# Query and key stacks of a two-layer attention kernel: part copies sent from SBUF to SBUF instead of through DRAM

## Chip, cores and metric

The kernel runs on one core of one Trainium2 chip. The metric is the device time of the whole launch in microseconds (us), the median of three runs.

## What is computed

The input is x with T = 1024 tokens and D = 256 features. There are two layers, each of the form x + attention(norm(x)) * silu(ffn(norm(x))).

```
layer 0: q = xn@Wq -> 16 heads x (q1,q2) of 16;  k = xn@Wk -> 4 kv heads x (k1,k2) of 16, rotary on all
         a_m = softmax(q_m k_m^T / 4 + causal mask), out = (a_1 - lam*a_2) v, group norm, @Wo
         ffn = mxfp4(xn) @ mxfp4(W)^T + bias
layer 1: q,k,v = xn@Wq, xn@Wk, xn@Wv -> 16 heads of 16, plain causal softmax attention, @Wo + bo
         ffn = gated mixture of 16 experts (top 4 of top 2 groups) of width 176, and a shared expert
```

A head's q1, q2, k1 or k2 is called a map here: 16 rows by 1024 tokens. Layer 0 has 32 query maps and 8 key maps, layer 1 has 16 and 16.

## The kernel before

**Stages.** The launch is a row of blocks, and each block ends when all engines have reached its end (a barrier; the wait shows in the profile at the line of the block's own statement: L231 for the first, L593 for an attention block, L981 for the middle one). The blocks are: the layer 0 projections (lines 231 to 393), the layer 0 attention (`attention`, 16 pairs of maps), `middle` (output projection, layer 0 ffn, second norm, layer 1 projections and routing), the layer 1 attention (8 pairs, the same function), and `experts`.

**Split parts.** Scores need fp32 accuracy from bf16 matmuls. Each fp32 projection value is cut into three bf16 parts (high, middle, low). The tile `stack0` (layer 1: `stack1`) holds for each map a column block of 1024 tokens and, in its partitions, six copies of 16 rows: for queries the parts 0, 1, 2, 0, 1, 0 (`QPARTS`), for keys the parts 0, 0, 0, 1, 1, 2 (`KPARTS`). One matmul over these 96 partitions gives all products of parts that count. Three more partitions hold the row maxima.

**Units.** The projections come in units (f, c): f is a group of 8 maps = 128 rows, c a half of the tokens. Layer 0 has ten units, in the order `UN`: the keys (f = 4) first, then queries f = 0 to 3, each with c = 0, 1. Layer 1 has eight (`UN1`). For each unit TensorE projects (L381) and swaps neighbouring rows with a permutation matrix `swp` (L371), VectorE multiplies with the rotary tables `rp` (L344, L346), GpSimd adds (L273), and ScalarE, VectorE and GpSimd cut the parts into a slot of `spl` (L302, L352, L305, L277; in layer 1 L1078, L1202, L1081, L1021). When the low part is done, the semaphore `lo_ok` rises.

**The way into the stack.** Everything that moves is a DMA from SyncE's queue, in program order. On `lo_ok` of a unit, `written` (L178) issues three DMAs from `spl` to a DRAM tensor (`part_scratch`, called `scr`; layer 1 `scr1`): 384, 256 and 128 KB, 768 KB in 1 KB rows. When both halves of a group are written, `gathered` (L182) reads the group back from DRAM into 96 partitions of the stack, with the rows and maps exchanged on the way: `near_maps` the first two maps (384 KB), `far_maps` the other six (1152 KB). In the block of the projections these reads are issued after units 2 and 3 for groups 4 and 0; the rest is issued during the attention's first pairs, from `late`, behind the three small DMAs of `rows` (L833). In layer 1 the groups 2 and 0 are read after the fourth unit and groups 3 and 1 during pairs 0 and 1. TensorE waits in `loaded` for what a pair needs.

**Other names.** `outputs` (L446, L447, L453, L454) copies the attention's results from SBUF to SBUF, 32 or 16 partitions at a time, and single rows with them. SLOTS = 8 slots of `spl` in layer 0, SPL = 5 in layer 1; ScalarE waits for the DMAs of a slot's last use (`unit_written`) before it writes the slot again.

Of the kernel before, what the change touches and what calls it, by code (L numbers as in the profile page):

```python
# [18 lines left out]
BF16 = mybir.dt.bfloat16  # L19
# [4 lines left out]
P = 128  # L24
# [48 lines left out]
def program(nc, x, wq, wk, wv, wo, lams, gnw, gnb, fw, fb, wq1, wk1, wv1, wo1, bo, gate,  # L73
# [46 lines left out]
    with ctx:  # L120
        ps = ctx.enter_context(nc.psum_tensor("ps", [P, 8, 512], F32))
        psb = ps[:, :, :].bitcast(BF16)
        scr = nc.dram_tensor("part_scratch", [5 * P, 6, T], BF16, kind="Internal").ap()
        scr1 = nc.dram_tensor("part_scratch1", [4 * P, 6, T], BF16, kind="Internal").ap()
# [29 lines left out]
        stk0 = [sem(f"stk0_{f}") for f in range(5)]  # L154
        stk1 = [sem(f"stk1_{f}") for f in range(4)]
        near0 = [sem(f"near0_{f}") for f in range(5)]
# [29 lines left out]
        def wait_written(sp, layer, f):  # L186

            for c in range(NC):
                sp.wait_ge(*unit_written(layer, (UN, UN1)[layer].index((f, c))))
# [4 lines left out]
        def near_maps0(sp, f):  # L194

            wait_written(sp, 0, f)
            gathered(sp, stack0, at0(f), scr, f, 0, 2, near0[f])

        def far_maps0(sp, f):

            gathered(sp, stack0, at0(f), scr, f, 2, 8, stk0[f])


        with ExitStack() as a:
# [10 lines left out]
            qf = sb("qf", [P, 2, 512], F32)  # L215
            lm = sb("lm", [P, 4, DH], F32)
# [13 lines left out]

# [1467 lines left out]
```

## Time and profile before

| | |
|---|---|
| median of three runs | 868.28 us (868.22 to 869.21) |
| the profiled execution: its own time, its span | 868.93 us, 867.2 us |
| mean granted TensorE clock | 0.92 |
| busy: TensorE, weight loads, VectorE, ScalarE, GpSimd | 762.9, 365.0, 529.4, 432.3, 430.6 us |
| DMA of the data queue | 69.15 MB in 60016 packets |
| writes to part_scratch | 18 of 384 KB, 18 of 256 KB, 18 of 128 KB |
| reads from part_scratch | 9 of 384 KB, 9 of 1152 KB |

The span runs from the first to the last instruction of the profiled execution; 1.7 us of its own time lie outside. Lines such as L178 are lines of the kernel. SPq is SyncE's issue of DMAs: its duration is the time for which the issue holds the queue, not the time of the transfer. PEq and POOLq are the sequencers of TensorE and GpSimd.

### The profile page before, as it was taken

Reading aid. Unit: us, or ns where it says so; the run is one execution under the profiler, and the core shown is the slowest. Engines: PE = TensorE matmul, PEld = TensorE weight load, DVE = VectorE, ACT = ScalarE, POOL = GpSimd, SP = SyncE. Lnnn points to the kernel's source line nnn. Section 1 sums busy time; section 2 is a strip of 40 time slices with the busy share of each in tenths; the row PEclk is TensorE's granted clock in tenths of the full one; section 3 lists DMA queues with packets and bytes.
Section 4 is the critical chain, followed back from the end, with each engine's and each line's share of the span. In section 5 each row is a group of like instructions: output and inputs, shape, how many; then the busy total and the mean of one; then the engine's idle time right before and its main releaser. Section 6 shows DMA issues by size and latency. Waiting matters only on the chain. (4 is left out here: it accounts for less than half of the span.)

```text
span 867.2 us, 12855 instructions
## 1 busy us (share of the span) xinstructions
PE 762.9 (88%) x3632; PEld 365.0 (42%) x3632; DVE 529.4 (61%) x1441; ACT 432.3 (50%) x922; POOL 430.6 (50%) x751
## 2 busy tenths in 40 slices
PE   3938999999999999965984889999669999999995
PEld 2322222222222223222651222322148888888884
DVE  3649787778777768223653867886035555555555
ACT  1431666666666556732141256666534555455552
POOL 1751566654244324321222123334276999799994
PEclk9985999999999999975996698999969999999997
DMA  5393630110020011012059552432221212122221
GB/s 182 130 299 87 154 87 15 43 43 14 20 63 15 21 40 38 21 44 60 1 179 261 129 141 66 126 98 69 87 87 43 66 60 67 52 62 71 62 64 55
DMA packets 60075, 69.83 MB, mean 81 GB/s; under 512 B 14904, under 2 KB 40857, under 8 KB 60010
## 3 DMA queue, kind: packets, MB, share of 16 engines
q1 hardware_dynamic: 60016, 69.15, 28.4%
q8 instruction: 24, 0.39, 0.2%
q14 instruction: 35, 0.29, 0.1%
HBM read 47.35 MB, written 15.47 MB: 72 GB/s over the span
## 5 line engine op out<-in xcount | busy, mean ns | idle before, releaser
L675 ACT ACTIVATE top<-ps 128x512 f32<-128x512 f32 (+3 forms) x384 | 171.0, 490 | 132.4 <-PE ps L622 132.2
L605 PE MATMUL ps<-mid 96*128 96x512 bf16 (+3 forms) x576 | 191.2, 356 | 29.0 <-PEq L981 11.8
L709 DVE CUSTOM_DVE_ANT_0 ps<-ps,keep 128x512 f32<-128x512 f32 (+3 forms) x384 | 184.2, 504 | 41.9 <-PE ps L605 41.2
L622 PE MATMUL ps<-mid 99*128 99x512 bf16 (+3 forms) x576 | 185.7, 338 | 9.2 <-ACT mid L675 6.3
L1450 PE MATMUL ps<-xp,wp 128*128 128x512 f32 (+1 forms) x600 | 149.6, 400 | 14.3 <-ACT wp L1502 8.8
L642 PE MATMUL ps<-top,mid 128*33 128x512 f32 (+3 forms) x768 | 161.6, 500 | 0.0
L622 PEld LDWEIGHTS ps<-mid 99*128 99x128 bf16 x576 | 54.3, 99 | 185.8 <-ACT top L675 103.0
L1450 PEld LDWEIGHTS ps<-xp,wp 128*128 128x128 f32 (+1 forms) x600 | 115.0, 192 | 40.3 <-ACT xp L1504 9.3
L791 POOL TENSOR_SCALAR_AFFINE_SELECT top<-top 128x128 f32<-128x128 f32 x256 | 71.5, 294 | 109.4 <-ACT top L675 107.0
L675 ACT ACTIVATE mid<-ps 128x512 f32<-128x512 f32 (+1 forms) x192 | 82.6, 492 | 69.9 <-PE ps L622 41.8
L713 DVE TENSOR_REDUCE top<-ps 128x1 f32<-128x512 f32 x128 | 88.4, 691 | 36.0 <-PE ps L605 35.5
L1622 DVE SCALAR_TENSOR_TENSOR a<-th,ps 128x512 f32<-128x512 f32 (+1 forms) x50 | 34.4, 688 | 91.1 <-ACT th L1520 91.1
L605 PEld LDWEIGHTS ps<-mid 96*128 96x128 bf16 x576 | 58.2, 102 | 75.3 <-issue 30.1
L1466 PE MATMUL ps<-gp,w2p 128*128 128x512 f32 (+1 forms) x300 | 77.7, 395 | 2.0 <-POOL gp L1572 2.0
L1552 POOL TENSOR_TENSOR wp<-top,wp 128x512 fp32r<-128x512 f32 (+1 forms) x50 | 64.6, 1293 | 27.9 <-ACT wp L1502 27.9
L1572 POOL TENSOR_TENSOR gp<-g,gp 128x512 fp32r<-128x512 f32 (+1 forms) x50 | 64.6, 1292 | 8.8 <-ACT gp L1533 2.6
L791 POOL TENSOR_SCALAR_AFFINE_SELECT mid<-mid 128x128 f32<-128x128 f32 x128 | 36.2, 293 | 63.3 <-ACT mid L675 60.1
L1533 ACT CAST gp<-g 128x512 fp32r<-128x512 f32 (+1 forms) x50 | 31.1, 622 | 68.3 <-DVE g L1631 68.3
L1466 PEld LDWEIGHTS ps<-gp,w2p 128*128 128x128 f32 (+1 forms) x300 | 57.0, 191 | 14.4 <-POOL gp L1572 2.5
L1568 POOL TENSOR_TENSOR w2p<-top,w2p 128x256 fp32r<-128x256 f32 (+1 forms) x50 | 57.5, 1151 | 2.7 <-ACT w2p L1530 2.7
L642 PE MATMUL ps<-mid 128*17 128x512 f32 (+3 forms) x384 | 55.0, 512 | 0.0
L713 DVE TENSOR_REDUCE mid<-ps 128x1 f32<-128x512 f32 x64 | 44.1, 689 | 16.2 <-PE ps L605 16.1
(199 smaller groups left out, 777.7 us busy)
## 6 DMA issues: line engine op xcount, KB each, us to landing
mid<-part_scratch SPq DMA_DIRECT2D x9, 1152.0 KB, 8.6
part_scratch<-top SPq DMA_DIRECT2D x18, 384.0 KB, 5.1
top<-in_w SPq DMA_DIRECT2D x16, 396.0 KB, 4.0
cw_s<-combine_rows SPq DMA_DIRECT2D x48, 128.0 KB, 3.0
part_scratch<-top SPq DMA_DIRECT2D x18, 256.0 KB, 5.2
mid<-part_scratch SPq DMA_DIRECT2D x9, 384.0 KB, 3.9
top<-inverse_scratch SPq DMA_DIRECT2D x12, 256.0 KB
top<-in_w SPq DMA_DIRECT2D x8, 384.0 KB, 5.4
```

The lines of the kernel that those rows point to most:

```text
L605: nc.tensor.matmul(ps[:, s_bank(turn), 0:w], queries(pair, m)[0:PARTS, i * P:(i + 1) * P], keys(pair, m)[0:PARTS, c * 512:c * 512 + w], st ...
L622: nc.tensor.matmul(ps[:, ST_BANK + n % AHEAD, 0:w], keys(pair, m)[0:STACK, j * P:(j + 1) * P], queries(pair, m)[0:STACK, q0:q0 + w], start ...
L642: nc.tensor.matmul(ps[r0:r0 + dv, ACC + c, q0 - 512 * c:512], v, pr[:, n % RING, 0:w], start=start, stop=stop).then_inc(multiplied, 1)
L675: nc.scalar.activation(pr[:, n % RING, 0:w], ps[:, ST_BANK + n % AHEAD, 0:w], ACT.Exp, scale=0.25).then_inc(p_ready, 1)
L709: ins = nc.vector.tensor_tensor_reduce(bank, bank, msk[:, 512 - w:512], -1.0 if low else 1.0, 3e38 if low else -3e38, ALU.add, ALU.min if ...
L713: ins = nc.vector.tensor_reduce(mx[:, m, i - 4, c:c + 1], bank, AX.X, ALU.max)
L791: nc.gpsimd.affine_select(out=square, in_=square, pattern=[[1, P]], compare_op=ALU.is_ge, fill=0.0, base=0, channel_multiplier=-1).then_in ...
L1450: last = nc.tensor.matmul(ps[0:r, bank + b, :], wp[:, b, pw, w + kk, 0:r], xp[:, px, kk, c * 512:(c + 1) * 512], start=j == 0 and kk == 0, ...
L1466: last = nc.tensor.matmul(ps[:, YB + kk, :], w2p[0:r, b, pw, kk * P:(kk + 1) * P], gp[0:r, b, pg, :], start=first and j == 0, stop=final a ...
L1552: nc.gpsimd.tensor_tensor(wp[:, b, 1, :, 0:r], w13[:, :, :, bass.ds(i * P, r)].rearrange("p w c n -> p (w c) n"), wp[:, b, 0, :, 0:r].bitc ...
L1568: nc.gpsimd.tensor_tensor(w2p[0:r, b, 1, :], w2s[0:r, bass.ds(i, 1), :].rearrange("p i d -> p (i d)"), w2p[0:r, b, 0, :].bitcast(F32), ALU ...
L1572: nc.gpsimd.tensor_tensor(gp[0:r, b, 1, :], g[0:r, b, :], gp[0:r, b, 0, :].bitcast(F32), ALU.subtract).then_inc(gl_ok, 1)
```

## The change

The DRAM tensors and the gathers are gone. `written` now sends six DMAs for each unit, one for each copy of a part: its 128 partitions go into 16 partitions by 8 maps of the stack, 1 KB for each row and map, 128 KB in all. A DMA walks the source's partitions in order, so the projection's rows must come as (row in the map, map) and not as (map, row). For this GpSimd reorders the columns of the weights once they are loaded (`regrouped`: one copy of 128 x 256 elements for the keys and four for the queries in layer 0, four in layer 1). The raw weights are loaded into tiles that are not in use yet (`r1`, `qf`, layer 1 `r11`). The rotary tables are loaded as 16 rows repeated for 8 maps, in two DMAs instead of one. The permutation matrix is made by VectorE from the identity (two copies of 128 x 64) instead of loaded. All waits for gathers become waits for the six DMAs of the units: TensorE waits for a whole group at the first pair that needs it, and SyncE waits for all units at the start of each attention (`early0`, `early1`) before it issues anything there.

```
-        scr = nc.dram_tensor("part_scratch", [5 * P, 6, T], BF16, kind="Internal").ap()
-        scr1 = nc.dram_tensor("part_scratch1", [4 * P, 6, T], BF16, kind="Internal").ap()
...
-            return scr_ok[slot], 48 * (before + v // SLOTS + 1)
+            return scr_ok[slot], 96 * (before + v // SLOTS + 1)
...
-        def written(sp, to, f, c, parts, is_key, done):
-            rows = to[f * P:(f + 1) * P, :, c * 512:(c + 1) * 512]
-            for first_row, width, part in ((0, 3, 0), (3, 2, 1), (5, 1, 2)):
-                if is_key:
-                    of = parts[:, part, :].unsqueeze(1).to_broadcast([P, width, 512])
-                else:
-                    of = parts[:, 0:width, :]
-                sp.dma_start(rows[:, first_row:first_row + width, :], of).then_inc(done, 16)
-        def gathered(sp, stack, at, of, f, lo, hi, done):
-            sp.dma_start(stack[0:PARTS, at + lo:at + hi, :],
-                         of[f * P + 16 * lo:f * P + 16 * hi, :, :].rearrange("(m r) n t -> (r n) m t", r=16)
-                         ).then_inc(done, 16)
+        def written(sp, stack, at, c, parts, is_key, done):
+            for n, part in enumerate(KPARTS if is_key else QPARTS):
+                sp.dma_start(stack[16 * n:16 * n + 16, at:at + 8, c * 512:(c + 1) * 512], parts[:, part, :]).then_inc(done, 16)
...
+        def by_row(w):
+            return w.rearrange("p k (m r) -> p k r m", r=16)
+        def regrouped(pool, to, of, f, done):
+            cols = slice(f * P, (f + 1) * P)
+            nc.gpsimd.tensor_copy(to[:, :, cols].rearrange("p k (r m) -> p k r m", r=16), by_row(of[:, :, cols])).then_inc(done, 1)
...
+            wk_raw = r1[:, 0, 0:KD * P].rearrange("p (k n) -> p k n", k=KD)
...
+            def turned(v):
+                return v[:, :].rearrange("p (a b m) -> p a b m", b=2, m=8)
...
-                    sp.dma_start(swp[:, :], swap).then_inc(ld_c, 16)
-                    for t, w in ((wk_s, wk), (wv_s, wv), (wq_s, wq)):
+                    for t, w in ((wk_raw, wk), (qf, wq), (wv_s, wv)):
-                    sp.dma_start(rp[:, :, :], rope.rearrange("m p t -> p m t")).then_inc(ld_r, 16)
+                    for m in range(2):
+                        sp.dma_start(rp[:, m, :], rope[m, 0:16, :].unsqueeze(1).to_broadcast([16, 8, T])).then_inc(ld_r, 16)
...
-                        written(sp, scr, f, c, spl[:, u % SLOTS, :, :], f == 4, scr_ok[u % SLOTS])
-                        if u == 2:
-                            near_maps0(sp, 4)
-                        if u == 3:
-                            near_maps0(sp, 0)
-                            far_maps0(sp, 0)
+                        written(sp, stack0, at0(f), c, spl[:, u % SLOTS, :, :], f == 4, scr_ok[u % SLOTS])
...  GpSimd, layer 0, after the norm's rstd
+                    pool.wait_ge(ld_w, 16 * 3)
+                    regrouped(pool, wk_s, wk_raw, 0, v_clr)
+                    for f in range(4):
+                        regrouped(pool, wq_s, qf, f, v_clr)
...  VectorE, layer 0
-                    dve.wait_ge(ld_c, 48)
+                    dve.wait_ge(ld_c, 32)
+                    for odd in range(2):
+                        nc.vector.tensor_copy(turned(swp)[:, :, odd, :], turned(idf)[:, :, 1 - odd, :]).then_inc(ids, 1)
...
-                            late(sp, pair)
+                        early(sp)
                         ahead(0)
...
+                wait_written(pe, 0, 4)
             if pair % 4 == 0:
-                pe.wait_ge(near0[pair // 4], 16)
-            if pair % 4 == 1:
-                pe.wait_ge(stk0[pair // 4], 16)
+                wait_written(pe, 0, pair // 4)
+        def early0(sp):
+            for f in range(4):
+                wait_written(sp, 0, f)
...
+            if pair % 4 == 0:
+                wait_written(pe, 1, 2 + pair // 4)
+                wait_written(pe, 1, pair // 4)
+        def early1(sp):
+            sp.wait_ge(comb_kept, 16)
+            for f in range(4):
+                wait_written(sp, 1, f)
...  middle: SyncE, then GpSimd
-                    sp.dma_start(wqk[:, :, n * D:(n + 1) * D], w.rearrange("(c p) n -> p c n", p=P)).then_inc(ldw, 16)
+                    sp.dma_start(r1[:, :, n * D:(n + 1) * D], w.rearrange("(c p) n -> p c n", p=P)).then_inc(ldw, 16)
-                    written(sp, scr1, f, c, spl[:, u % SPL, :, :], f >= 2, scr_ok[u % SLOTS])
-                    if u == EARLY - 1:
-                        near_maps1(sp, 2)
-                        near_maps1(sp, 0)
-                        far_maps1(sp, 2)
-                        far_maps1(sp, 0)
+                    written(sp, stack1, 8 * f, c, spl[:, u % SPL, :, :], f >= 2, scr_ok[u % SLOTS])
+                pool.wait_ge(ldw, 64)
+                for f in range(4):
+                    env["regrouped"](pool, wqk, r1, f, v_clr)
                 pool.wait_ge(stats, 3)
```

## Rows read from the trace of the kernel before

**Rows 1.** Stages: us, busy of PE, PEld, DVE, ACT, POOL, clock, DMA share, GB/s
```profile
0.00:63.70 63.70, 34.36 (x108) 18.16 (x109) 29.57 (x63) 21.33 (x38) 30.34 (x30) 0.94 0.64 200
378.80:470.50 91.70, 60.71 (x248) 37.95 (x249) 40.51 (x152) 23.86 (x50) 22.37 (x35) 0.76 0.38 107
```

**Rows 2.** Timeline, end of the first block and start of attention 0
```profile
55.03 1.15 POOL L277 TENSOR_TENSOR top<-top 128x512 bf16<-128x512 f32 x1
...
63.72 4.45 PE L605 MATMUL ps<-mid 96*128 96x128 bf16 x14 [11.05 <-PEq L231]
```

**Rows 3.** Timeline of SyncE's queue, layer 0 (start, us held, line)
```profile
32.31 7.67 SPq L178 DMA_DIRECT2D part_scratch<-top  x9
...
47.23 15.85 SPq L178 DMA_DIRECT2D part_scratch<-top  x18
```

**Rows 4.** The same writes to DRAM grouped by line, 30 to 64 us
```profile
DMA to landing us min/median/max: 2.5/5.2/9.7
```

**Rows 5.** Stretches, columns as in rows 1: queue saturated; narrow copies alone
```profile
57.00:63.00 6.00, 0.00 (x0) 0.00 (x0) 0.00 (x0) 0.00 (x0) 0.00 (x0) 0.50 1.09 384
...
549.40:553.20 3.80, 3.80 (x24) 1.15 (x21) 3.18 (x8) 2.72 (x6) 0.00 (x0) 1.00 0.13 28
```

**Rows 6.** Timeline of SyncE's queue, middle block
```profile
440.32 10.26 SPq L178 DMA_DIRECT2D part_scratch<-top  x12
...
456.60 13.03 SPq L178 DMA_DIRECT2D part_scratch<-top  x12
469.68 0.31 SPq L1001 DMA_DIRECT2D combine_rows<-top  x1
```

**Rows 7.** Timeline, end of the middle block and start of attention 1
```profile
459.10 2.26 POOL L1021 TENSOR_TENSOR top<-top 128x512 bf16<-128x512 f32 x2 [0.80 <-ACT top L1081]
...
470.51 4.45 PE L605 MATMUL ps<-mid 96*128 96x128 bf16 x14 [11.76 <-PEq L981]
```

**Rows 8.** SBUF-to-SBUF DMAs by line: issue min/median/max ns, and time to landing
```profile
L453 SPq DMA_DIRECT2D keep<-keep x24: 507/589/593, 509.5 to 627.5; - x24
DMA to landing us min/median/max: 1.9/2.1/10.1
...
L454 SPq DMA_DIRECT2D keep<-keep x32: 585/589/1180, 510.0 to 628.2; - x32
DMA to landing us min/median/max: 1.7/1.8/9.7
```

**Rows 9.** Timeline of SyncE's queue: one load, and two copies back to back
```profile
4.88 0.47 SPq L241 DMA_DIRECT2D mid<-in_fw  x1
...
549.64 0.59 SPq L454 DMA_DIRECT2D keep<-keep  x1
550.27 0.59 SPq L453 DMA_DIRECT2D mid<-keep  x1
```

**Rows 10.** Timeline of SyncE's queue, pairs 1 to 4 of attention 0
```profile
95.67 2.32 SPq L833 DMA_DIRECT2D mid<-top  x3
...
114.12 2.21 SPq L833 DMA_DIRECT2D mid<-top  x3
...
132.59 1.78 SPq L833 DMA_DIRECT2D mid<-top  x3
...
151.04 1.78 SPq L833 DMA_DIRECT2D mid<-top  x3
```

**Rows 11.** Timeline, GpSimd around the new copies, and TensorE's first projection
```profile
18.15 3.96 PE L381 MATMUL ps<-keep,top 128*128 128x512 f32 x8
...
24.38 1.26 POOL L273 TENSOR_TENSOR top<-top 128x512 f32<-128x512 f32 x1 [11.30 <-DVE top L346]
...
404.43 1.05 POOL L1013 TENSOR_TENSOR top<-top 128x4 f32<-128x4 f32 x1 [4.50 <-DVE top L1129]
```

**Rows 12.** One GpSimd line with one input, by line; one VectorE row of layer 0
```profile
L803 POOL TENSOR_SCALAR top<-top x5: 614/614/616, 93.9 to 167.6; 128x512 f32<-128x512 f32 x5
...
35.71 1.67 DVE L352 TENSOR_TENSOR top<-top 128x512 f32<-128x512 f32 x1 [0.37 <-POOL top L277]
```

More of the change, by code:

```diff
@@ L152, in program @@
         dqw = sb("dqw", [P, 2, D], BF16, mid)
-        stk0 = [sem(f"stk0_{f}") for f in range(5)]
-        stk1 = [sem(f"stk1_{f}") for f in range(4)]
-        near0 = [sem(f"near0_{f}") for f in range(5)]
         unit_near = sem("unit_near")
@@ L330, in _ @@
                                                 ALU.subtract, ALU.mult).then_inc(normed, 1)
-                    dve.wait_ge(ld_r, 80)
+                    dve.wait_ge(ld_r, 96)
                     for n in range(2):
@@ L369, in swapped @@
                     def swapped(u):
+                        if u == 0:
+                            pe.wait_ge(ids, 3)
                         pe.wait_ge(qs_ok, u + 1)
@@ L379, in _ @@
                         w, o = (wk_s, 0) if f == 4 else (wq_s, f * P)
+                        if c == 0:
+                            pe.wait_ge(v_clr, 2 if f == 4 else 3 + f)
                         for k in range(KD):
@@ L393, in _, with attention @@
                             last.then_inc(v_mm, 1)
-        def attention(layer, stack, vall, N, loaded, late):
+        def attention(layer, stack, vall, N, loaded, early):
             first = layer == 0
@@ L877, in loaded0 @@
                 pe.wait_ge(unit_near, 16)
-                pe.wait_ge(near0[4], 16)
-            if pair == 4:
-                pe.wait_ge(stk0[4], 16)
+                wait_written(pe, 0, 4)
             if pair % 4 == 0:
-                pe.wait_ge(near0[pair // 4], 16)
-            if pair % 4 == 1:
-                pe.wait_ge(stk0[pair // 4], 16)
-        def late0(sp, pair):
-            if pair == 0:
-                far_maps0(sp, 4)
-            if pair < 3:
-                near_maps0(sp, pair + 1)
-                far_maps0(sp, pair + 1)
+                wait_written(pe, 0, pair // 4)
+        def early0(sp):
+            for f in range(4):
+                wait_written(sp, 0, f)
         o0, combined0, last_inverses0, last_inverted0, last_scaled0, last_combined0 = attention(
-            0, stack0, v0, 16, loaded0, late0)
+            0, stack0, v0, 16, loaded0, early0)
         mid[1] = 0
@@ L897, in program @@
         stack1 = sb("stack1", [P, 32, T], BF16, mid)
-        def near_maps1(sp, f):
-            wait_written(sp, 1, f)
-            gathered(sp, stack1, 8 * f, scr1, f, 0, 2, unit_near)
-        def far_maps1(sp, f):
-            gathered(sp, stack1, 8 * f, scr1, f, 2, 8, stk1[f])
         middle(nc, locals())
@@ L915, in loaded1 @@
             if pair == 0:
-                pe.wait_ge(unit_near, 16 + 3 * 16)
-            if pair == 4:
-                pe.wait_ge(unit_near, 16 + 5 * 16)
-            if pair % 4 == 1:
-                pe.wait_ge(stk1[2 + pair // 4], 16)
-                pe.wait_ge(stk1[pair // 4], 16)
-        def late1(sp, pair):
-            if pair == 0:
-                sp.wait_ge(comb_kept, 16)
-            if pair < 2:
-                near_maps1(sp, (3, 1)[pair])
-                far_maps1(sp, (3, 1)[pair])
+                pe.wait_ge(unit_near, 16 + 16)
+            if pair % 4 == 0:
[5 more added lines that the diff above has]
+                wait_written(sp, 1, f)
         o1, combined1, last_inverses, last_inverted, last_scaled, _ = attention(
-            1, stack1, v1, 8, loaded1, late1)
+            1, stack1, v1, 8, loaded1, early1)
         mid_c.close()
@@ L940, in middle @@
         env[n] for n in ("idf", "mv", "st6", "rst", "ve", "mhalf", "wo_s", "gnc"))
-    v1, stack1, scr1, idb, comb = (env[n] for n in ("v1", "stack1", "scr1", "idb", "comb"))
+    v1, stack1, idb, comb = (env[n] for n in ("v1", "stack1", "idb", "comb"))
     st6o, dqa, dqw, row_stats = (env[n] for n in ("st6o", "dqa", "dqw", "row_stats"))
@@ L978, in middle @@
         UN, scr_ok, unit_written, unit_near = (env[n] for n in ("UN1", "scr_ok", "unit_written", "unit_near"))
-        written, near_maps1, far_maps1 = env["written"], env["near_maps1"], env["far_maps1"]
+        written = env["written"]
         EARLY = 4
@@ L1288, in _ @@
                         pe.wait_ge(ldw, 64)
+                        pe.wait_ge(v_clr, 2 + 4)
                     if t >= 3:
```

11 lines of the change are left out of this document (4 added, 7 removed).

## Prediction

> **What bounds the kernel now.** I read the stages first, then both ends of the two stages that the change touches, and only then the queue that does the moving. The projections of layer 0 take 63.7 of 867.2 us and the middle block 91.7 us [rows 1]; everything else keeps its instructions. In the first block the last unit's low part is done at 55.03 + 1.15 = 56.18 us, and yet the first matmul of attention 0 starts at 63.72, after 11.05 us in which TensorE had nothing [rows 2]. The compute engines wait there for one thing, SyncE's queue: its last write to the scratch is issued at 47.23 + 15.85 = 63.08 [rows 3]. The queue itself is held by the transfers. 18 DMAs take 15.85 us, 0.88 us each, where a load is issued in 0.47 us [rows 3, 9]; the DMA engines are full at 384 GB/s while nothing else runs [rows 5], and a write lands 5.2 us after its issue [rows 4]. The same picture stands at the end of the middle block: last part done at 459.10 + 2.26 = 461.36, queue done at 469.68 + 0.31 = 469.99, TensorE starts at 470.51 after 11.76 us of idleness [rows 6, 7]. So about 7 us and 8.5 us of the time are queue alone. Both are on the path, and a change that shortens or lengthens the queue moves the end of the launch one for one, until the units' own times (56.2 and 461.4) become the bound.
>
> **What the change removes.** All reads from scratch, 1536 KB for each of nine groups, go. Three groups' worth of them, or parts, stand in the queue before the barriers; the others lie in the attention. Those in the attention are covered: the row maxima go out at 95.67, 114.12, 132.59 and 151.04, so the pairs take 18.45, 18.47 and 18.45 us, the first two with gathers behind the maxima and the third without [rows 10]. I count no gain there. The traffic ahead of the barriers halves, so the full DMA engines are no longer what holds the queue, if the new writes go at the old rate.
>
> **What it adds: six issues for each unit in place of three.** There are 60 in layer 0 and 48 in layer 1, all of 128 KB from SBUF to SBUF. The trace has no such DMA. The nearest rows are the SBUF-to-SBUF copies of the attention, which hold the queue for 0.59 us in the median whatever they carry, 32 KB (L453) or 2 KB (L454) [rows 8], and start 550.27 - 549.64 = 0.63 us apart back to back [rows 9]. The other neighbour is a load with 128 partitions, 0.47 us, or 0.51 with the same 0.04 us between two [rows 9]. I take 0.63, as source and target are both in SBUF, and keep 0.51 as the lower bound. Upward I take 0.70, the copy's price and some of what a fuller queue adds.
>
> Layer 0: the first unit comes at 32.31 and the units come every (56.18 - 32.31) / 9 = 2.65 us. Six issues take 6 x 0.63 = 3.8 us, so after the first unit the queue never runs empty. It ends at 32.31 + 60 x 0.632 = 70.2 where it ended at 63.1: +7.1 us. The first pair needs only the first four units, issued by 32.31 + 24 x 0.632 = 47.5, so it waits for the barrier and not for data.
>
> Layer 1: the first four units need 24 issues, 15.2 us from 440.32 to 455.5, and are through before the fifth comes at 456.60 [rows 6]. The other four take 15.2 us from there, to 471.8, and the combine rows 0.3: 472.1 against 469.99, +2.1 us.
>
> **The regroupings.** A GpSimd instruction with one input over 512 elements takes 614 ns [rows 12]. For 256 elements read with a stride the bounds are 0.3 us (half of it) and 1.2 us (four times that); I take 0.6. Layer 0: GpSimd sits idle for 11.30 us before 24.38 [rows 11], so from 13.08; the key weights are ready at 13.7 (at most 14.3) and TensorE first wants them at 18.15 [rows 11]; all five are done at 16.1, at most 19.1. Middle: GpSimd sits idle for 4.50 us before the power at 404.43 [rows 11], which is on the path; four copies take 2.4 us, at most 4.8. So 0, and +0.3 us at the upper bound. If the cover were gone it would be 2.4 us. There is a second way to pay. A VectorE row next to GpSimd work, both reading SBUF, took 1.67 us [rows 12], and tiny VectorE steps of the group norm now run beside the four copies. I enter +0.2 us for it, between 0 and 1.
>
> **The rest.** The swap matrix is no longer loaded, one issue of 0.47 us less ahead of VectorE's start, and two copies of 128 x 64 elements more on VectorE; together about 0, between -0.3 and +0.3. The second rotary DMA is one issue of 0.47 us in a queue whose tables are first used after 18.15. SyncE's wait for all units at the start of an attention stands ahead of the row maxima, which were issued about 14 us after the attention's start; the last unit lands about 5 us after its issue at most, if that is as slow as the full queue's median [rows 4], so nothing behind it is late. ScalarE's wait for a slot comes eight units after the slot's last use, five in layer 1: the tightest is the last unit there, whose slot was issued until 440.32 + 18 x 0.632 = 451.7 and is wanted shortly before 459. Both hold only as long as the transfers keep up with the queue. TensorE's granted clock is already 0.50, its lower level of 1.2 GHz, in the wait before attention 0 [rows 5], so a longer wait adds its length and no lower clock.
>
> **Sum.** 7.1 + 2.1 + 0.2 = 9.4 us. The profiled execution takes 868.93 us by its own time (span 867.2), the median is 0.65 less: 878.3 for it, 877.7 for the median; I say 878.
>
> **Rival 1: the narrow target is the bound.** Each DMA writes into 16 partitions only. L453 does that with 32 KB and lands 2.1 us after issue; L454 beside it moves 2 KB and lands after 1.8 [rows 8]. 30 KB more for 0.3 us is 100 GB/s, a quarter of the 384 of [rows 5]. In the stretch that holds those copies alone the engines are busy 13% of the time for 28 GB/s, 215 GB/s at full share [rows 5], though such short copies hardly overlap. At 100 GB/s a DMA takes 1.3 us, at 215 it takes 0.6, just the issue interval. It decides from 0.63 us, that is below 207 GB/s. At 1.3 us the 60 DMAs of layer 0 need 78 us from 32.3, to 110, and the queue ends 5 to 10 us ahead of that, as far as it ran ahead of its landings before [rows 4]: about +39. The 48 of layer 1 need 62 us from 440.3, to 503, or about +20 with the wait ahead of the row maxima: about 927 in all. Against it: consecutive DMAs go to different partitions, so engines that have drifted apart can use several targets at once. A half-way 0.9 us gives 32.3 + 54 - 6 = 80 (+17) and 440.3 + 43 - 3 = 480 (+10): 895.
> The Trainium skill (SBUF — State Buffer, "Door 1: The DMA port swizzle") says that a transfer's rate depends on how many of 16 ports its partitions reach, and that 16 partitions reach four, measured at 104 GB/s. By that a DMA would take 1.26 us, as in the slow form of this rival; the landing times of this trace agree (100 GB/s).
>
> **Rival 2, the other sign: the queue is freed.** Without gathers and with half the traffic the queue may go at the price of an issue alone, and that may be smaller than the copies'. At 0.51 us layer 0 ends at 32.3 + 30.6 = 62.9 (-0.2) and layer 1 at 456.6 + 12.2 + 0.3 = 469.1 (-0.9): 867, no difference that can be told. It decides from 0.51 down. At 0.45 us layer 0 ends at 59.3 and layer 1 at 467.7: -3.8 and -2.3, 862. For it: a load's price is close to this. Against it: every SBUF-to-SBUF row stands at 0.59 us.
>
> **Rival 3: nothing to see.** Rival 2 at 0.51, or a gain in one layer and a loss in the other.
>
> **Chances and range.** A run of this kernel can tell 0.2%, 1.7 us, from no change. The forecast (issue-bound, 0.57 to 0.70 us): 0.52. Its own range is 872 (0.57: 66.5 and 470.6, +4.1) to 884 (0.70: 74.3 and 474.2, +15.4). Rival 1: 0.27, two thirds of it below 900, as the drift helps. Rival 2 with a gain: 0.12. Rival 3: 0.09. The range 867 to 900 leaves out the faster cases and the slow third of rival 1. Faster 0.12, same 0.09, slower 0.79.
>
> **What the profile after would show.** If I am right: in SyncE's queue 60 writes from 32.3 to about 70, one row, each held 0.59 us, and 24 from 456.6 to 472; landing within 3 us; TensorE's first L605 matmuls at about 70.8; DMA share well below full with the queue still busy. Rival 1: issues held for 1 us and more, landing after 5 to 12 us, DMA share near full at 100 to 200 GB/s. Rival 2: issues of 0.47 us or less and TensorE starting before 63.7. The regroupings are right if the power at L1013 comes no later after VectorE's L1129 than before. The prediction fails above all if the price of an issue depends on the shape in a way that these rows don't show, or if narrow targets share a path.

## Result: 2.6% slower, and where the 21 us lie

The changed kernel takes 891.12 us (888.76 to 893.13) against 868.25 us of the kernel before on the same chip: a ratio of 1.0261, 95% interval 1.0233 to 1.0288. The forecast was 878. Its direction held and its size did not: the loss is 22.9 us and not 9.7.

The profiled execution after has a span of 888.7 us, 21.5 more than before. I cut both executions at the same four events: the first score matmul of attention 0, the first part transfer of layer 1, the first score matmul of attention 1, and the first gather of the experts.

| stretch | before | after | difference |
|---|---|---|---|
| start to attention 0 | 63.72 | 83.87 | +20.2 |
| attention 0 and the middle block up to the first part transfer | 376.60 | 377.97 | +1.4 |
| part transfers of layer 1 to attention 1 | 30.19 | 37.14 | +7.0 |
| attention 1 to the first gather of the experts | 159.35 | 153.15 | -6.2 |
| experts | 237.34 | 236.57 | -0.8 |

The +1.4 of the second row says little: the same stretch takes 375.8 us in the execution of run 10 below and 378.2 in that of run 12.

Stretches of the kernel after, with the columns of [rows 1] and of [rows 5]: the block of the projections, the middle block, the time in which only the queue is left, and attention 1:

```profile
0.00:83.70 83.70, 34.42 (x108) 18.14 (x108) 31.04 (x65) 21.33 (x38) 33.34 (x34) 0.84 0.85 123
399.80:498.70 98.90, 60.82 (x248) 38.10 (x248) 41.22 (x152) 24.00 (x50) 24.59 (x39) 0.74 0.48 65
55.00:83.00 28.00, 0.00 (x0) 0.00 (x0) 0.79 (x3) 1.70 (x4) 2.38 (x2) 0.55 1.16 132
498.70:652.00 153.30, 137.05 (x776) 39.07 (x776) 105.18 (x340) 88.64 (x208) 47.19 (x165) 0.91 0.36 92
```

TensorE's own work is what it was (34.42 us against 34.36 in [rows 1]); the block is longer by waiting. From 55 to 83 us the DMA engines are full (share 1.16), as they were in [rows 5], but they move 132 GB/s where they moved 384. Busy DMA engines at a third of the rate are the main finding: the share alone would say that nothing changed.

The timeline after, end of the first block and start of attention 0, which answers to [rows 2]:

```profile
53.31 4.07 POOL L267 TENSOR_TENSOR top<-top 128x512 bf16<-128x512 f32 x3
53.59 29.15 SPq L168 DMA_DIRECT2D mid<-top  x30
...
83.87 2.72 PE L601 MATMUL ps<-mid 96*128 96x128 bf16 x9 [30.01 <-PEq L220]
```

The last 30 transfers take 29.15 us to issue, 0.97 each, and TensorE idles for 30.01 us where it idled for 11.05. Grouped by line, all 60 of layer 0 (issue min/median/max in ns, first and last start, then issue to landing), which answers to [rows 4]:

```profile
L168 SPq DMA_DIRECT2D mid<-top x60: 597/627/1962, 33.5 to 82.0; - x60
...
DMA to landing us min/median/max: 3.4/14.7/16.8
```

The first transfer lands 3.4 us after its issue, the median one 14.7. While the queue has room the issues go out 0.65 us apart, as the forecast had it, and the transfers land 1.06 us apart (36.88, 37.99, 39.05, 40.12). One issue is held for 0.98 us at 45.28, but the next 14 go out 0.64 to 0.69 us apart again. From 55.5 us on, with 16 or 17 transfers under way, nearly every issue is held until a transfer has landed. The last is issued at 81.95 and lands at 96.46.

SyncE's queue in the middle block, which answers to [rows 6], and attention 1's start, which answers to [rows 7]:

```profile
461.84 35.78 SPq L168 DMA_DIRECT2D mid<-top  x48
497.66 0.45 SPq L972 DMA_DIRECT2D combine_rows<-top  x1
514.54 1.83 SPq L829 DMA_DIRECT2D mid<-mid  x3
```
```profile
484.88 2.26 POOL L995 TENSOR_TENSOR top<-top 128x512 bf16<-128x512 f32 x2 [5.06 <-ACT top L1055]
...
498.98 6.34 PE L601 MATMUL ps<-mid 96*128 96x128 bf16 x18 [18.70 <-PEq L957]
```

The last transfer lands at 512.63. SyncE's wait for all units ends there, and VectorE has the row maxima ready at 513.10, so this wait doesn't hold them up. They go out at 514.54, 15.6 us after the attention's start and not 14.2 (484.66 against 470.51 before); the profile puts the last 1.4 us to the DMA of the combine rows, which stood behind the transfers, but doesn't show why. The delay cost no time that can be seen: the next maxima go out 31.1 us after the attention's start, and 30.9 before.

The slots of `spl` ran out as well. ScalarE waits 5.1 us for the transfers of a slot in the middle block:

```profile
483.70 0.59 ACT L1052 CAST top<-ps 128x512 bf16<-128x512 f32 x1 [5.11 <-DMA mid<-top]
```

The last low part is done at 484.88 + 2.26 = 487.14, 25.3 us after the first transfer where it was 21.0 before. The queue ends 11 us later still, so this wait is covered too.

**The start.** The first part transfer goes out at 33.52, 1.2 us later than in [rows 3]. Timelines of 12 to 20 us, the kernel after and then the kernel before:

```profile
13.10 3.09 POOL L185 COPY top<-top 128x256 f32<-128x256 f32 x5
13.25 4.05 DVE L321 TENSOR_SCALAR top<-keep 128x256 f32<-128x256 f32 x8 [2.21 <-POOL keep L251]
```
```profile
13.19 2.67 DVE L329 TENSOR_SCALAR top<-keep 128x256 f32<-128x256 f32 x8 [2.21 <-POOL keep L267]
```

The five regroupings take 3.09 / 5 = 0.62 us each, and VectorE's eight normalisations beside them take 4.05 us and not 2.67. The transposes behind them start 1.15 us later (15.86 against 14.71). In all executions of full kernels the eight normalisations take 4.05 or 4.06 us where the copies run beside them and 2.67 where they don't. At the first transfer the difference is blurred: the kernel before and runs 2, 8, 9 and 12, whose code is the same up to there, have it between 32.31 and 33.22.

**What came back.** In the kernel before, SyncE issues the gathers of groups 3 and 1 in the first two pairs of attention 1, and right behind them, as in every pair of this attention, three loads of expert weights (`in_w`, 1176 KB). Its timelines and its stretches there:

```profile
503.30 1.01 SPq L182 DMA_DIRECT2D mid<-part_scratch  x2
504.35 1.02 SPq L841 DMA_DIRECT2D top<-in_w  x2
505.41 0.50 SPq L844 DMA_DIRECT2D top<-in_w  x1
```
```profile
517.12 0.58 ACT L685 COPY mid<-ps 64x512 f32<-64x512 f32 x1 [2.48 <-DMA keep<-mid]
```
```profile
506.00:511.00 5.00, 5.00 (x34) 1.57 (x32) 3.85 (x12) 3.66 (x10) 2.29 (x8) 1.00 1.06 234
511.00:516.00 5.00, 4.48 (x26) 1.32 (x22) 4.34 (x15) 2.55 (x5) 0.44 (x2) 1.00 1.02 284
516.00:521.40 5.40, 3.16 (x13) 0.58 (x14) 0.97 (x5) 2.46 (x5) 0.44 (x2) 0.61 0.01 3
521.40:530.00 8.60, 8.60 (x39) 2.54 (x38) 5.19 (x16) 4.18 (x11) 2.68 (x10) 0.65 0.47 150
```

Gathers and weights fill the DMA engines from 506 to 516, the small output copies behind them land up to 10 us after their issue [rows 8], ScalarE waits for the buffer that they empty, TensorE is idle for 2.2 of 5.4 us, and its granted clock falls to its lower level, 0.50, from 517.2 to 527.5 (so the means of 0.61 and 0.65 in the last two stretches). The row maxima of attention 1's pairs are 16.7, 20.0 and 18.5 us apart before, and 15.5, 16.2 and 15.9 after, where the weight loads go on as they were.

### The profile page after: what moved, and what is told of

The parts are those of the page before. It is cut to its first block and busy times, and to the rows that moved or that the text cites. A ratio compares the mean times of both kernels' runs of the same rounds, so it can differ in the third digit from the quotient of the medians.

```text
span 888.7 us, 12906 instructions
## 1 busy us (share of the span) xinstructions
PE 758.5 (85%) x3632; PEld 363.2 (41%) x3632; DVE 531.4 (60%) x1443; ACT 431.8 (49%) x922; POOL 435.7 (49%) x760
## 5 line engine op out<-in xcount | busy, mean ns | idle before, releaser
L1425 PE MATMUL ps<-xp,wp 128*128 128x512 f32 (+1 forms) x600 | 149.2, 399 | 14.5 <-ACT wp L1477 8.8
L1527 POOL TENSOR_TENSOR wp<-top,wp 128x512 fp32r<-128x512 f32 (+1 forms) x50 | 64.6, 1292 | 27.7 <-ACT wp L1477 27.7
L1508 ACT CAST gp<-g 128x512 fp32r<-128x512 f32 (+1 forms) x50 | 31.1, 622 | 68.5 <-DVE g L1606 68.5
L1441 PEld LDWEIGHTS ps<-gp,w2p 128*128 128x128 f32 (+1 forms) x300 | 56.2, 188 | 14.2 <-POOL gp L1547 2.5
```

The lines of the kernel that those rows point to most:

```text
L1425: last = nc.tensor.matmul(ps[0:r, bank + b, :], wp[:, b, pw, w + kk, 0:r], xp[:, px, kk, c * 512:(c + 1) * 512], start=j == 0 and kk == 0, ...
L1441: last = nc.tensor.matmul(ps[:, YB + kk, :], w2p[0:r, b, pw, kk * P:(kk + 1) * P], gp[0:r, b, pg, :], start=first and j == 0, stop=final a ...
L1527: nc.gpsimd.tensor_tensor(wp[:, b, 1, :, 0:r], w13[:, :, :, bass.ds(i * P, r)].rearrange("p w c n -> p (w c) n"), wp[:, b, 0, :, 0:r].bitc ...
```

## Experiments

**1. The shapes by themselves.** A kernel of DMAs alone, from a 128-partition SBUF tile with 1 or 2 KB for each partition, and no computation:

```
for i in range(18): sp.dma_start(dst[16n:16n+16, 8 maps, 512], src[:, 0:512])      # the kernel's shape and order
for i in range(8):  sp.dma_start(dst[0:32, 8 maps, 512], src as [128, 2, 512])     # and 0:16, 0:64, all 128, DRAM
```

> Only DMAs, no attention: series of equal transfers from one SBUF tile of 128 partitions, one series after the other; the output is zeros. Theory (the narrow target is the bound): 128 KB into 16 partitions land 1.0 to 1.1 us apart in the order of the kernel and 1.2 us apart in the order 0, 2, 1, 3, 4, 5 of the copies; the same split over two queues lands under 0.9 us apart; 256 KB land 2.4 us apart when all go into partitions 0 to 15, 2.0 us when they alternate between partitions 0 to 15 and 64 to 79, 1.2 us for 32 and for 64 partitions alike, 0.7 us for 128 partitions; from DRAM into 16 partitions about 2.1 us, as from SBUF. Rival A (any SBUF-to-SBUF transfer is slow, the source counts): 256 KB into 128 partitions land 2.1 us apart too, and from DRAM into 16 partitions 0.7 us. Rival B (the issue is the bound): everything of 128 KB lands 0.65 us apart.

Stretches of it (DVE and POOL, clock, DMA share, GB/s), in this order: the kernel's shape; 256 KB to 16 partitions; to 32; to 64; to 128; from DRAM to 16:

```profile
8.00:24.00 16.00, 0.00 (x0) 0.00 (x0) 1.00 1.11 117
70.00:90.00 20.00, 0.00 (x0) 0.00 (x0) 1.00 1.06 117
123.00:138.00 15.00, 0.00 (x0) 0.00 (x0) 1.00 1.04 130
141.00:157.00 16.00, 0.00 (x0) 0.00 (x0) 1.00 1.00 131
160.00:165.00 5.00, 0.00 (x0) 0.00 (x0) 1.00 1.02 381
173.00:190.00 17.00, 0.00 (x0) 0.00 (x0) 1.00 0.95 123
```

The kernel's shape lands every 1.06 us with nothing else in the program, and the issue is not what holds it. By line, the kernel's shape and the same 128 KB to all 128 partitions:

```profile
L41 SPq DMA_DIRECT2D dst<-src x18: 579/608/687, 3.6 to 14.7; - x18
...
DMA to landing us min/median/max: 3.4/7.0/10.4
```
```profile
L79 SPq DMA_DIRECT2D dst<-src x12: 472/601/603, 190.9 to 197.9; - x12
...
DMA to landing us min/median/max: 2.0/2.1/2.1
```

Same bytes, same issue of 0.6 us; one falls behind by 7 us in 18 transfers ((14.7 + 10.4 - 3.6 - 3.4) / 17 = 1.06 us each), the other never (0.64 us apart, the issue). So the narrow target is the bound, and that the source lies in SBUF is not, since DRAM to 16 partitions is as slow (2.06 us for 256 KB). Two things that I had counted on don't help: 256 KB always to partitions 0 to 15 take 2.27 us each, and alternating between 0 to 15 and 64 to 79 2.17; and from two queues at once the pair together gives the same 1.06 us per transfer, where I had expected less than 0.9. In the order 0, 2, 1, 3, 4, 5 of the copies it is 1.15 us (1.2 expected). The expected 1.2 us for 256 KB into 32 and 64 partitions didn't come: they take 2.02 and 1.92.

**2 and 3. One layer at a time.** The kernel before with the direct transfers in layer 1 alone, and in layer 0 alone:

```
+ direct(sp, stack1, 8 * f, c, ...)       - written(sp, scr1, f, c, ...), near_maps1, far_maps1      # 2
+ written(sp, stack0, at0(f), c, ...)     - near_maps0, far_maps0; layer 1 as before                 # 3
```

> The kernel before with the change made in layer 1 alone. Theory (the slow copies hold the middle block's queue about 7 us longer, and the gathers that are gone had cost attention 1 about 6.5 us in its pairs 2 and 3): 867 to 870 us, attention 1 at least 5 us shorter than before, its start 6 to 8 us later. Rival (the gathers in the attention were covered, as the prediction has it; attention 1 got shorter for another reason, such as the clock): 874 to 876 us.

> The changed kernel with layer 1 put back to the DRAM scratch, layer 0 direct. Theory (nearly all of the loss is layer 0's queue, ending 19 to 20 us later, and its start 1.2 us later): 888 to 892 us, attention 0 starting at 83 to 85 us, attention 1 as long as before. Rival (layer 1 costs its share too, as in the prediction's 7 to 2): 882 to 886 us.

Layer 1 alone gives 873.61 us, ratio 1.0049 (1.0035 to 1.0062), layer 0 alone 887.17, ratio 1.0211 (1.0185 to 1.0238). Together that is +22.6 us, and the whole change is +22.9: the parts add up. In layer 1 alone the stretch of the part transfers is 38.6 us (30.2 before) and attention 1 takes 153.5 (159.3): a loss of 8.4 and a gain of 5.8 that mostly hide each other. Attention 1 was shorter as the theory had it, but it starts 11.1 us later and not 6 to 8, 2.7 of it from before the first part transfer, and so the time lies above the theory's 867 to 870. Run 3 lies just below its 888 to 892. Its attention 0 starts at 84.31, as expected; its attention 1 takes 157.0 us and not as long as before, although its gathers are back; why is open.

**4. The regroupings after the normalisation.**

```
+ pool.wait_ge(normed, NT)
  regrouped(pool, wk_s, wk_raw, 0, v_clr)
```

> The changed kernel, but GpSimd starts its weight copies in layer 0 only when VectorE has written all eight normalised tiles. Theory (the copies hold VectorE back while both read SBUF, and that is the first unit's 1.2 us): first write issued at about 32.4 us instead of 33.5 and a time 1.0 to 1.4 us under the changed kernel's. Rival (the later start comes from the loads): no change, 33.5 us.

The timeline of its queue and its GpSimd copies:

```profile
32.53 3.89 SPq L168 DMA_DIRECT2D mid<-top  x6
```
```profile
16.07 2.85 POOL L185 COPY top<-top 128x256 f32<-128x256 f32 x5 [2.94 <-DVE top L322]
```

The normalisations take 2.67 us again and the transposes start at 14.78, 1.1 us earlier. The first transfer goes out at 32.53, 1.0 us earlier, and attention 0 starts at 82.80, 1.07 us earlier. The time is 890.83 (ratio 1.0249, 1.0227 to 1.0270) against a ratio of 1.0261 (1.0233 to 1.0288): the microsecond is in the trace and can't be told in the times.

**5 and 11. More shapes.**

> Only DMAs, one shape after another, no computation; 256 KB each unless said. The first such run gave 2.0 to 2.2 us per 256 KB for targets of 16, 32 and 64 partitions and 0.68 for 128 partitions or DRAM. Theory (each of the 16 engines writes into its own share of the target's partitions, one packet after another, and is slow when several packets in a row go to one partition): 64 to 64 partitions in rows of 4 KB near 2, 16 to 16 in rows of 16 KB near 2, 16 source partitions spread over 128 target partitions fast (0.7), 128 to 128 in 1 KB packets fast. Rival (the count of packets or their 1 KB size is what costs): long rows into 16 partitions fast, 128 to 128 in 1 KB packets as slow as the kernel's. Second rival (source and target rows that don't match are what costs): 64 to 64 fast, 16 spread over 128 slow. From DRAM to 96 partitions: near 0.9 per 384 KB by the kernel before's rate in its busiest stretch, where theory one would want about 3. Issued by GpSimd, the kernel's own shape lands every 1.06 us as from SyncE.

> Only DMAs again, 8 of each shape. So far, in GB/s: 16 partitions on either side 98 to 125, 64 to 64 197, DRAM to 64 213, 128 to 128 from 347 (1 KB packets) to 387, and, out of line, 128 source partitions to 64 or 32 target partitions 137 and 130. Theory (the narrower side sets the rate, and a target partition that takes rows of several source partitions costs besides): 32 to 32 and DRAM to 32 100 to 150, 96 to 96 near 250 to 300, DRAM to 96 near 249 whatever the length of the row, 128 to 64 in 1 KB packets 137 or less. Rival (the packet's length is what makes 128 to 64 slow): 128 to 64 in 1 KB packets about half of that.

The rates from the times between landings, with those of experiment 1 (K is 1024 bytes, GB is 10^9):

| source to target partitions | us for KB | GB/s |
|---|---|---|
| 16 to 16; 16 to 128 | 2.63; 2.57 for 256 | 100; 102 |
| 128 to 16 (kernel's shape) | 1.06 for 128 | 124 |
| DRAM to 16 | 2.10 for 256 | 125 |
| 32 to 32; DRAM to 32 | 1.37; 1.25 for 256 | 192; 209 |
| 64 to 64; 64 to 128; DRAM to 64 | 1.33; 1.30; 1.23 for 256 | 197; 201; 213 |
| 128 to 32; 128 to 64 in 2 KB rows | 2.02; 1.92 for 256 | 130; 137 |
| 128 to 32; 128 to 64 in 1 KB rows | 0.86; 0.80 for 128 | 153; 163 |
| 16 to DRAM | 2.51 for 256 | 105 |
| 96 to 96 in 1 KB rows | 0.75 for 192 | 262 |
| DRAM to 96, 384 KB in 1 KB rows; in 4 KB rows; 768 KB | 1.54; 1.35; 3.13 | 255; 292; 252 |
| 128 to 128 in 1 KB rows; 2 KB rows | 0.76; 0.68 for 256 | 347; 387 |

The first theory of run 5 falls: 16 partitions spread over 128 are as slow as 16 to 16, though every packet goes to a partition of its own, and 64 to 64 is not near 2. So do both rivals. Against the first, long rows into 16 partitions are slow and 128 to 128 in 1 KB rows is fast. What the second had forecast came (64 to 64 fast, 16 over 128 slow), but its reason, rows that don't match, doesn't hold: 16 to 16 match and are slow, 64 to 128 don't and are as fast as 64 to 64. What fits is that the side with fewer partitions sets the rate, reading or writing: 16 give 100 to 125 GB/s, 32 and 64 about 200, 96 from 252 to 292, 128 more than 340. GpSimd as the issuer changes nothing (0.53 us held, a landing every 1.04 us). Out of line stay 128 partitions into 32 or 64, at 130 to 163 GB/s; run 11 shows that a longer row doesn't help them. Both its theory (137 or less for 128 to 64 in 1 KB rows, 100 to 150 for 32 partitions) and its rival (half of 137) miss that. DRAM to 96 partitions in the gathers' 1 KB rows takes 1.54 us for 384 KB, where I had expected near 0.9. Why 128 into 32 or 64 is slow is open, and what is left of the idea of unlike rows would fit these two shapes.
The Trainium skill (SBUF — State Buffer, "Door 1: The DMA port swizzle") gives 104 GB/s for 16 partitions, 189 for 32 and 196 for 64, because 32 and 64 reach the same eight ports. The runs agree with 100, 192 and 197 for equal widths; 128 to 16 went at 124, above the 104, and here the measurement decides.
The Trainium skill (SBUF — State Buffer, "Can I just issue two DMAs to hit both halves?") says that two transfers to different halves don't add up. Run 1 agrees: 5% from alternating.

**6, 7 and 10. The same issues to a wide target.** In the changed kernel the 108 part transfers go to 128 rows of DRAM, and the stack holds ones:

```
- sp.dma_start(stack[16 * n:16 * n + 16, at:at + 8, c * 512:(c + 1) * 512], parts[:, part, :])
+ sp.dma_start(aside[at // 8, n, :, c * 512:(c + 1) * 512], parts[:, part, :])       # 6 and 10: all six; 7: n = 0 alone
```

> The changed kernel, but each of the 108 part transfers goes to 128 rows of a DRAM buffer in place of 16 partitions of the stack (same number, bytes, source and order; the stack holds ones, put there by five transfers before the first part is ready; nothing reads the DRAM buffer, so the result isn't the reference's). My theory: the transfer's price is what missed, so the queue here runs at the 0.65 us of an issue, attention 0 starts near 33.5 + 60 x 0.65 + the last low part = 72 to 74 in place of 84, and attention 1 starts 17 to 20 earlier in all; with attention 1 at 153: 868 to 873. Rival (the SBUF source or the count of 108 is the cause, wherever they go): 885 to 891.

> As the run before it, but only the first of the six part transfers of each unit is made (18 in all), to DRAM: what is left of the stage when the queue has next to nothing to do. Theory: the queue alone holds the stage back; the split parts are then ready at their own pace and attention 0 starts at 52 to 60, attention 1 some 15 us earlier again than with all six: 845 to 858. Rival (the computation of the parts is nearly as slow as six issues, so that fewer transfers give little): within 3 us of the run before it.

> The run in which the 108 part transfers go to DRAM rows, but the five transfers that put ones into the stack come after layer 0's last part transfer, so that they no longer hold up the first ones. Its time says nothing (about 25 us of those five lie open before attention 0); its layer 0 queue is to be read. Theory: an issue to DRAM rows costs 0.49 us, so a unit's six take 2.95 us, as long as the engines take for a unit (2.9 us in the run with one transfer of six); nothing backs up, landings stay within 2 us of the issue, and the last part transfer is issued 27 to 30 us after the first. Rival (sixty issues hold the stage back wherever they go): 36 us or more after the first, as I predicted for the change.

Run 6 took 877.03 us (ratio 1.0085, 1.0069 to 1.0100), above what my theory gave, and below its rival; attention 0 starts at 77.8 and not at 72 to 74. Its trace says why, and that it can't be read in layer 0: the five transfers that put the ones there land until 53.5 us, the first part transfer stands behind them and lands 18.6 us after its issue, and the slots run out. Its layer 1 has no such thing: 48 transfers in 27.9 us, against 35.8 in the changed kernel. Run 7 took 853.92 (ratio 0.9822, 0.9806 to 0.9838). In layer 0 the ones cost it too: the eighth unit's low part is done at 57.39, 5.9 us after the seventh's, as ScalarE waits for a slot for the ninth first, and attention 0 starts at 62.08 and not before 60, as I expected. In layer 1 the stretch of the part transfers takes 22.5 us where the kernel before takes 30.2: that is what a queue with nothing to do is worth there, 7.7 us. Its attention 1 takes 152.9 us.

Run 10 mends run 6. By line and as a timeline, layer 0's queue:

```profile
L169 SPq DMA_DIRECT2D part_scratch<-top x60: 319/449/1856, 33.0 to 63.8; - x60
...
DMA to landing us min/median/max: 1.7/1.8/3.5
```
```profile
33.02 31.20 SPq L169 DMA_DIRECT2D part_scratch<-top  x60
```

Sixty issues of the same bytes take 31.20 us, 0.52 each, and end at 64.2; every transfer lands within 3.5 us. The last unit is done at 56.9, so the issues still set the end of the stage, 7 us behind it, but no transfer does. The last is issued 30.8 us after the first, just above the 27 to 30 of the theory and well below the rival's 36; the run's time, 899.38 us, says nothing. With the narrow target the issues end at 82.7, 18.5 us later. Not all of this is the transfer's: an issue to DRAM holds the queue for 0.45 us, one to SBUF for 0.61 even where the target is wide (0.60, run 1). Sixty issues to SBUF 0.65 us apart, held by nothing else, would end at 33.5 + 60 x 0.65 = 72.5 (an estimate). So some 8 us of the 18.5 go with the dearer issue and the later start, and 10 with the slow transfers. The term on which the forecast rested is not refuted by run 10; it would have been near the truth had the transfers been fast. The kernel with a wide target in SBUF, which would show this directly, wasn't run.

**8, 9 and 12. A version that is faster than both.** The forecast's step on the gathers had failed, so I moved them in the kernel before. Run 8 issues the far gathers of the first groups behind the barrier. Run 9 also spreads those of groups 3 and 1 over pairs 0 to 3. Run 12 sends all far gathers of layer 1 in pieces of two maps, each awaited by its own pair:

```
- near_maps1(sp, 0); far_maps1(sp, 2); far_maps1(sp, 0)       # after the fourth unit
+ near_maps1(sp, 0)
+ def early1(sp): far_maps1(sp, 2); far_maps1(sp, 0)          # 8, 9; in layer 0 far_maps0(sp, 0) the same way
- if pair < 2: near_maps1(sp, (3, 1)[pair]); far_maps1(sp, (3, 1)[pair])
+ if pair <= 3: for f in (3, 1): near_maps1(sp, f) if pair == 0 else two maps of f         # 9
+ pair 0: maps 4 to 7 of groups 2 and 0; pair 1: near maps of 3 and 1; pairs 2 to 4: two maps of each    # 12
```

> The kernel before, with the far gathers that stand in the SyncE queue between the writes (group 0 of layer 0; groups 2 and 0 of layer 1) moved behind the barrier, to the attention's start. Their maps are first wanted a pair later. Theory: bytes leave the stage that is bound by the queue, 0.75 MB x 1.3 in layer 0 (about 3 us at 384 GB/s) and 2 x 1.2 MB in layer 1 (up to 6 us), and lie beside attention work that doesn't need the queue yet: 859 to 865. Rival (the gathers then collide with the first outputs and rows of the attention, as groups 3 and 1 did in layer 1): 866 to 872.

> The run with the late far gathers, and in the second attention the gathers of groups 3 and 1 no longer go out whole in pairs 0 and 1: their first two maps go in pair 0, and then two maps of each in pairs 1, 2 and 3 (pieces of 384 KB); group 4's far gather of the first attention stands where the kernel before has it. Theory: in the kernel before those gathers held back the outputs of attention 1 (pairs 1 to 3 at 20.0 and 18.5 us against 16.2 and 15.9 in the changed kernel), so attention 1 takes 153 to 155 us in place of 160: 859 to 862. Rival (the 6 us come from something else in the changed kernel, such as the later start or the clock): attention 1 stays at 159 to 160 us and the time at 865 to 867.

> The run with the gathers of attention 1 spread out lost 5.7 us of TensorE's time in its first pair: pair 1's scores, which start some 10 us into pair 0, waited for the far gathers of groups 2 and 0 as a whole (2.4 MB sent at the barrier). Here all far gathers of layer 1 go as pieces of two maps (384 KB), and each pair waits for its own piece alone: pair 1's two pieces at the barrier, those of pairs 2 and 3 in pair 0, the near maps of groups 3 and 1 in pair 1, then one piece of each a pair. Theory: the wait goes, and attention 1 takes 153 to 154 us in place of 156.5: 856 to 858. Rival (the gathers cost TensorE its pace in pair 0 by their traffic, not by the wait): 859 to 861.

| run | time, us | ratio (95%) | attention 1 starts | attention 1 takes |
|---|---|---|---|---|
| 8 | 865.79 | 0.9953 (0.9939 to 0.9967) | 467.36 | 159.9 |
| 9 | 859.88 | 0.9899 (0.9868 to 0.9930) | 464.26 | 156.5 |
| 12 | 864.67 | 0.9945 (0.9924 to 0.9965) | 466.57 | 160.5 |

Run 8 lies between its theory (859 to 865) and its rival (866 to 872): attention 1 starts 3.2 us earlier and takes as long as before. Run 9 is 1.0% faster than the kernel before, and 3.5% faster than the changed one. Its row maxima are 16.2 and 15.9 us apart in pairs 1 to 3, as in the changed kernel, so the gathers were what held those pairs back. Attention 1 takes 156.5 us and not 153 to 155. The timeline of its first pair:

```profile
479.18 1.11 PE L604 MATMUL ps<-mid 96*128 96x128 bf16 x4 [5.68 <-DMA mid<-part_scratch]
```

TensorE waits 5.7 us for the far gathers, which pair 1's scores want 10 us into pair 0 and not one pair later, as I had assumed. Run 12 removes that wait (its trace has none for the scratch there), and yet loses what run 9 had gained in attention 1, and misses the expected 856 to 858. Its pieces of pair 4 meet that pair's outputs and inverses. Timeline, and stretches around it:

```profile
558.62 0.35 DVE L478 RECIPROCAL keep<-keep 128x32 f32<-128x32 f32 x1 [3.40 <-DMA keep<-mid]
```
```profile
550.00:555.00 5.00, 4.99 (x34) 1.41 (x33) 4.21 (x14) 3.19 (x9) 2.15 (x9) 1.00 0.99 287
555.00:560.00 5.00, 2.86 (x14) 0.70 (x12) 1.60 (x7) 1.96 (x4) 0.67 (x3) 0.95 0.48 143
560.00:565.00 5.00, 5.00 (x19) 1.44 (x19) 3.49 (x12) 2.60 (x5) 0.71 (x4) 0.50 0.21 63
565.00:570.00 5.00, 5.00 (x21) 1.47 (x19) 2.46 (x11) 2.66 (x6) 1.04 (x4) 0.53 0.01 1
```

It is the picture of 506 to 530 us in the kernel before again: 5 us of full DMA engines, small copies late, TensorE idle for 2.1 us, and its clock at 0.50 for the 10 us that follow. The maxima of these two pairs are 21.6 us apart where 15.9 is the pace. That the last two pieces alone do this was not tried by itself; in pairs 2 and 3 the same pieces beside the same weight loads cost nothing (16.2 us or less between the maxima).

## Why the prediction missed

**What bounds the kernel.** Right. The queue sets the end of both stages, one for one: the units of layer 0 are done at 56.18 before and 57.38 after, and the difference of 1.2 is the start's, while the queue's end moved by 19.7 us. In layer 1 run 7 gained 7.7 us without the queue, of the 8.5 that I had read there.

**Six issues for each unit: the step that failed.** The issue price held: 0.65 us apart where I had 0.63. That "the full DMA engines are no longer what holds the queue, if the new writes go at the old rate" did not hold: the writes go at a third of it (124 to 132 GB/s against 384). The price of a transfer into 16 partitions stood nowhere in the sum. A transfer takes 1.06 us at first and 0.97 to 0.99 later, 1.01 in the mean, so a unit takes 6.1 us and not 3.8. The term for layer 0 should have been 33.5 + 3.4 + 59 x 1.01 = 96.5 for the last landing, less 14.5 us by which the queue runs ahead of its landings: 82.0 for the last issue. The queue ended at 82.7, +19.7 and not +7.1; about half of this would have come from the later start and 0.65 us for an issue alone. In layer 1 it ended 36.3 us after its first transfer, against 29.7 before: +6.6 and not +2.1.

**Rival 1 was the case.** Its condition, below 207 GB/s, is met at 124. Of its two forms neither is the size: at 1.3 us it gave 927, because it let the queue run only 5 to 10 us ahead of its landings, where it ran 14.5 ahead, and because the price is 1.06. The half-way 0.9 us gave +17 and +10, 895 in all. With +19.7 and +6.6 its total comes within 4 us of the measured time, but partly by luck: it has no 6.2 us of gain in attention 1. I gave it 0.27 on one argument, that consecutive DMAs to different partitions overlap. Run 1 measured that: 5%. The two rows of [rows 8] had spoken for it, 100 GB/s from the 30 KB more; run 5 finds 16 to 16 at 100 GB/s. The rows carried the answer, and I set an unmeasured hope against them.

**Rival 2 by its own terms** would have been right for another target: to DRAM rows an issue costs 0.45 us, 60 of them 31.2, and the queue ends at 64.2 (run 10), where the rival's 0.51 us had 62.9.

**The removed gathers: wrong in layer 1.** I judged both attentions by layer 0's pairs, which do go on at 18.46 us with gathers behind them. In attention 1 whole gathers cost 6.2 us between the two kernels. Two things differ there: a pair has 12 small output copies where it has 8 in attention 0, and 1176 KB of expert weights are loaded in each pair right behind the gathers, where attention 0 loads none. Which of them makes the gathers cost was not tried. Three executions with whole gathers in pairs 0 and 1 take 157.0 to 159.9 us for attention 1 (the kernel before and runs 3 and 8), six without any in it 152.9 to 153.5 (the changed kernel and runs 2, 4, 6, 7 and 10). Without this gain the span would have grown by 27.7 us.

**The regroupings.** 0.62 us each, as taken (0.6). I had seen the second way to pay, but for the middle block alone, and priced it at 0.2. In layer 0, where it had no term, it cost 1.15 us, because the eight normalisations are on the path at that point and went from 0.33 to 0.51 us each. Run 4 takes 1.1 of it back. In the middle block the power (L987 after, L1013 before) comes 0.1 us after VectorE's step and so no later than before, as expected; VectorE's two small copies beside the regroupings (L1095, L1096) take 0.37 and 0.52 us where they took 0.17 each, some 0.5 us on the path.

**The rest.** SyncE's wait for all units was free in layer 0 (maxima 14.2 us after the start, before and after) and in layer 1, but there by 0.5 us only: I had a landing time of 5 us at most and it was 15.9. ScalarE's wait for a slot, which I had as covered as long as the transfers keep up with the queue, came to 5.1 us in layer 1 and stayed hidden behind the queue's end. The clock was at its lower level, 0.50, from 56.4 us on before and from 57.7 after, and until 23.4 and 25.0 us after the first matmul of attention 0.

## What to carry to other kernels

Price a DMA by its narrower side, source or target, and by its issue, and take the larger: in these runs 16 partitions gave 100 to 125 GB/s, so that 128 KB cost 1.06 us and its issue 0.6. A detour through DRAM with 128 rows in and 96 out moved more bytes in less time. And 5 to 10 us of full DMA engines beside small copies on the path can cost more than the idle time that shows: buffers come free late, TensorE runs dry for 2 us, and its clock is at its lower level for 10 us more. Spreading the transfers in pieces took this away in run 9 and brought it back in run 12, so where the pieces go has to be read from a trace.

## What the runs showed of the chip

- A busy share of 1.0 or more on the DMA engines says nothing of the rate: 117, 132 and 381 GB/s all show as full (1.11, 1.16 and 1.02).
- Spread over partitions on one side only is worth nothing: 16 to 128 partitions goes at 102 GB/s, as 16 to 16.
- 128 partitions into 64 (137 to 163 GB/s) is slower than 64 into 64 (197). Not explained.
- The queue of one engine runs about 15 us, or 16 transfers of 128 KB, ahead of its landings (81.95 issued, 96.46 landed), which hides the start of a shortage: issues are held one after the other only from 22 us after the first transfer on (33.5 and 55.5).
